# Filling TensorE with identity transposes at the start of a fused AdaLN block, with the gate modulation, one statistic and one exponential moved

## The chip, the core and the metric

The kernel runs on one core of a Trainium2 chip. The metric is the device time of one execution in microseconds (us), as the median of several runs. TensorE (PE) multiplies matrices, PEld is its loading of weights, VectorE is DVE, ScalarE is ACT, GpSimd is POOL, and SP issues most of the DMAs.

## What is computed

The input x has 8 samples of 256 rows with 128 features. It goes through eight layers of linear attention with a feed-forward part, and then through a mixture of 8 experts (top 2) with a shared one. Both halves are modulated by a small product of the condition c.

```python
mod = (silu(c) @ wmod).reshape(8, 6, 1, 128)      # shifts, scales and gates
sa, ca, ga, sb, cb, gb = the six parts of mod
h = layernorm(x) * (1 + ca) + sa                  # the input of the first layer
for layer in range(8):
    q, k, v = h @ Wq + bq, h @ Wk + bk, h @ Wv + bv
    Q, K = elu(q) + 1, elu(k) + 1
    V = Q * sum(K * v) / (Q * sum(K) + eps)       # the sums run over the rows of a sample
    h1 = layernorm(gelu(V @ Wo + bo) + h)
    h = layernorm(gelu(gelu(h1 @ Wf1 + bf1) @ Wf2 + bf2) + h1)
x = x + ga * h
out = x + gb * mixture(layernorm(x) * (1 + cb) + sb)
```

## The kernel before, in words

The 2048 rows are cut into four chunks of 512 (two samples each). Features lie on the partitions for the products, rows for the norms, so each norm is a set of four 128x128 transposes to rows, statistics and normalization on DVE, a reciprocal root on POOL (`rstd`, L1013), and four transposes back. All of it is fp32; from the fourth chunk on, the q, k and v products are made of three products of split operands.

The layers run as a software pipeline of slots (`slots`, L223). In slot s, chunk s mod 4 of its layer makes its k, q and v products (index `a` in the code), while chunk s-1 makes its denominators, its output product and first sum (`b`), chunk s-2 its feed-forward part (`f`) and chunk s-3 its last norm (`d`). Slots 0 to 2 are written out and are called the fill here; a hardware loop then runs four slots per iteration. Each engine has its own `slot` function, a list of work in a fixed order with semaphore waits. What belongs to the start alone (the input norm "I" of each of the four chunks) is passed to the slots as named extras, which a slot runs at a named place.

Around the change, engine by engine:

- **PE** (L340 to L351): ten products of zeros (L343), then with the modulation weights there `modulate(ps_y, (0, 1))`, four identity transposes (`keep_awake`, L326, whose output nobody reads), the four transposes of chunk 0's input (`first_to_fm(0)`, L319), then a wait for the gate weights and the four gate products `modulate(ps_d, (2, 3, 4, 5))` (L336). Slot 0 makes k, q and v (L360) and then `first_to_fm(1)`. Slot 1 makes k, q and v of chunk 1 (k waits for the keys of chunk 0, q for `elu_q`, v for `kv_ready`), `first_to_fm(2)`, the output product of chunk 0 (L466) and twelve identity transposes. Slot 2 starts with the transposes of y1 and chunk 2's products.
- **ACT** (L791 on): `first_norm(c)` (L768) scales and shifts chunk c's input to xs; a slot makes `lden` (L803) and `dd` (L812) for chunk s-1 and the exponentials `ek` (L808) and `eq` (L815) for chunk s, in the order lden, ek, dd, eq; then come the gelus (L821, L827), which need another activation table.
- **DVE** (L1215 on): before slot 0, statistics of chunks 0, 1 and 2 (L1117) and the normalization (L1153) of chunks 0 and 1. A slot makes `nck` (L1229), `vt` (L1240, from dd and nck), `mk` (L1250), the keys `kk` (L1258), `mq` (L1263), `elu_q_sb` (L1271), `kv_full` (L1212) and `rk` (L1290). In slot 0 the extra "before the last norm", ahead of bk1 and mk, is `first_stats(3)`; in slot 1 the same place holds `third_norm` (normalization of chunk 2, then the variance of chunk 3).
- **POOL** makes `kpos` and `qk` (L1037, L1039) once `elu_q_sb` is there, and the sum y1 (L1033) once ACT has g1.

The extras before the change read:

```python
slots(pe, slot, {"middle": lambda: first_to_fm(1)}, ...
slots(dve, slot, {"before the last norm": lambda: first_stats(CH - 1)}, ...
```

Of the kernel before, what the change touches and what calls it, by code (L numbers as in the profile page):

```python
# [7 lines left out]
ACT = mybir.ActivationFunctionType  # L8
# [10 lines left out]
CH = NB * L // G  # L19
# [12 lines left out]
def adaln_block(nc, x, w_qkv, w_o, w_f1, w_f2, v_a, v_bo, v_ln1, v_bf1, v_bf2, v_ln2, c_t, w_mod,  # L32
                w_router, w_unit, ident_in, select_in, lower_in, out):

    with ExitStack() as ctx:
        def sb(name, shape, dt=F32):
            return ctx.enter_context(nc.sbuf_tensor(name, shape, dt))

        def sem(name):
            return ctx.enter_context(nc.semaphore(name))  # L40
# [23 lines left out]
        lden, dd = sb("lden", [P, G]), sb("dd", [P, G])  # L64
# [14 lines left out]
        c_eps, c_lneps, c_half = sb("c_eps", [P, 1]), sb("c_lneps", [P, 1]), sb("c_half", [P, T])  # L79
# [34 lines left out]
        ps_k, ps_q, ps_v, ps_f0, ps_f1, ps_b, ps_d, ps_y = bank  # L114
# [9 lines left out]
        def gates(i):  # L124
# [5 lines left out]
        ld = {k: sem(f"ld_{k}") for k in ("const", "ct", "mod", "gates", "moe", "wqkv", "va", "wo", "vbo", "vln1",  # L130
                                          "wf1", "vbf1", "wf2", "vbf2", "vln2")}
# [9 lines left out]
        lden_ready, dd_ready, v_ready = sem("lden_ready"), sem("dd_ready"), sem("v_ready")  # L141
# [37 lines left out]
        def rows_of(k, n):  # L179

            return hf[n][:].rearrange("p (t d) -> p t d", t=T) if k == "I" else xh[k][:]
# [8 lines left out]
        def splits_next(s, c):  # L190

            return c == CH - 1 and not (isinstance(s, int) and s == NI - 1)

        def has(n):

            return not isinstance(n, int) or 0 <= n < NI
# [10 lines left out]
        def run(extra, place):  # L207

            if extra and place in extra:
                extra[place]()  # L210
# [12 lines left out]
        def slots(eng, one_slot, *extras):  # L223

            extras = extras + (None,) * (CH - 1 - len(extras))
            for s in range(CH - 1):
                one_slot(s, s % CH, s // CH, extras[s])
            with eng.Fori(0, LAYERS - 1) as i:  # L230
                for j in range(CH):
                    s = CH - 1 + j
                    one_slot(i * CH + s, s % CH, i + s // CH)
            one_slot(NI - 1, CH - 1, LAYERS - 1)
# [79 lines left out]
        def _(pe):  # L314
            def transposes(out_bank, src, done):

                for j in range(T):
                    t = src[:, j, :] if len(src.shape) == 3 else src[:, j * P:(j + 1) * P]
                    mm = nc.tensor.transpose(out_bank[:, j * P:(j + 1) * P], t, ident[:])  # L319
                mm.then_inc(done, 1)  # L320


            def keep_awake(n, out_bank):

                for _ in range(n):
                    nc.tensor.transpose(out_bank[:, 0:P], ident[:], ident[:])  # L326

            def first_to_fm(c):
                pe.wait_ge(normed["I"], c + 1)
                if c == CH - 1:  # L330
                    pe.wait_ge(mod_copied, 2)
                transposes(first_bank[c], rows_of("I", c), to_fm["I"])

            def modulate(out_bank, ms):
                for m in ms:
                    mm = nc.tensor.matmul(out_bank[:, m * NB:(m + 1) * NB], wmod[:, m * D:(m + 1) * D], sct[:],  # L336
                                          start=True, stop=True)
                mm.then_inc(mod_mm, 1)
# [6 lines left out]
            pe.wait_ge(ld["mod"], 16)  # L345
            pe.wait_ge(silu_c, 1)
            modulate(ps_y, (0, 1))
            keep_awake(4, ps_v)
            first_to_fm(0)
            pe.wait_ge(ld["gates"], 16)  # L350
            modulate(ps_d, (2, 3, 4, 5))  # L351

            def slot(s, c, l, extra=None):
                a, b, f, d = s, s - 1, s - 2, s - 3
# [139 lines left out]
            def second_fill():  # L494
                pe.wait_ge(mod_copied, 1)
                keep_awake(12, ps_y)

            slots(pe, slot, {"middle": lambda: first_to_fm(1)},
                  {"behind the products": lambda: first_to_fm(2), "before ff2": second_fill},
                  {"behind the products": lambda: first_to_fm(CH - 1)})  # L500

# [1 line left out]
            last = NI - 1  # L503
# [248 lines left out]
        def _(act):  # L752
# [19 lines left out]
            def split_qkv_hi(l):  # L772
                act.wait_ge(ld["wqkv"], 16 * l + 16)
                wait(act, v_mm, CH * l)
                nc.scalar.activation(wqkv_hi[:], wqkv[:], ACT.Copy).then_inc(wq_hi_ready, 1)
# [8 lines left out]
            def last_norm(c, d):  # L784
                act.wait_ge(to_fm["D"], d + 1)
                if (c - 3) % CH == 0:
                    act.wait_ge(ld["vln2"], 4 * d + 16)
                nc.scalar.activation(xs[(c - 3) % CH][:], ps_d[:], ACT.Identity,
                                     bias=vln2[:, 1:2], scale=vln2[:, 0:1]).then_inc(x_ready, 1)

            def slot(s, c, l, extra=None):  # L791
                a, b, f, d = s, s - 1, s - 2, s - 3
                if has(d):
                    act.wait_ge(ff2_mm, d + 1)
                    if (c - 3) % CH == 0:
                        act.wait_ge(ld["vbf2"], 4 * d + 16)
                    nc.scalar.activation(g2[:], ps_f0[:], ACT.Gelu_apprx_tanh, bias=vbf2[:, 0:1]).then_inc(g2_ready, 1)  # L797
                run(extra, "start")
                if (has(a) or has(b)) and not (isinstance(s, int) and s <= 1):
                    nc.scalar.preload_act_table_set(LN_SET)  # L800
                if has(b):
                    act.wait_ge(q_ready, b + 1)
                    nc.scalar.activation(lden[:], qk[:], ACT.Ln, bias=c_eps[:, 0:1]).then_inc(lden_ready, 1)  # L803
                if has(a):
                    act.wait_ge(k_mm, a + 1)
                    if c == 0:
                        act.wait_ge(ld["va"], 4 * a + 16)
                    nc.scalar.activation(ek[:], ps_k[:], ACT.Exp, bias=va[:, 0:1]).then_inc(ek_ready, 1)  # L808
                if has(b):
                    act.wait_ge(lden_ready, b + 1)  # L810

                    nc.scalar.activation(dd[:], lden[:], ACT.Exp, bias=c_lneps[:, 0:1], scale=-1.0).then_inc(dd_ready, 1)  # L812
                if has(a):
                    act.wait_ge(q_mm, a + 1)
                    nc.scalar.activation(eq[:], ps_q[:], ACT.Exp, bias=va[:, 1:2]).then_inc(eq_ready, 1)  # L815
                run(extra, "before the gelus")
                if has(b):
                    act.wait_ge(wo_mm, b + 1)
                    if (c - 1) % CH == 0:
                        act.wait_ge(ld["vbo"], 4 * b + 16)  # L820
                    nc.scalar.activation(g1[:], ps_b[:], ACT.Gelu_apprx_tanh, bias=vbo[:, 0:1]).then_inc(g1_ready, 1)  # L821
                for j in range(FJ):
                    if has(f):
                        act.wait_ge(ff1_mm, 4 * f + (2, 3, 1, 4)[j])
                        if j == 0 and (c - 2) % CH == 0:
                            act.wait_ge(ld["vbf1"], 4 * f + 16)
                        nc.scalar.activation(hid[:, j, :], ps_ff[j][:], ACT.Gelu_apprx_tanh,  # L827
                                             bias=vbf1[:, j:j + 1]).then_inc(h_ready, 1)
                    if j == 0:
                        run(extra, "after the first gelu")  # L830
                    if j == 1:
                        run(extra, "middle")
                    if j == 3:
                        run(extra, "before the last norm")
                    if j == 3 and has(a) and splits_next(s, c):
                        split_qkv_hi(l + 1)
                    if j == 3 and has(d) and has(b) and has(s + 1):
                        last_norm(c, d)
                        if has(s + 1):
                            act.wait_ge(v_mm, d + 1)  # L840
                            nc.scalar.activation(xs_hi[(c - 3) % CH][:], ps_d[:], ACT.Identity,
                                                 bias=vln2[:, 1:2], scale=vln2[:, 0:1]).then_inc(x_hi_ready, 1)
                run(extra, "end")
# [111 lines left out]
            for i in range(CH * U):  # L955
# [17 lines left out]
                if i == U + 5:  # L973
                    act.wait_ge(to_fm["D"], NI)
                    nc.scalar.activation(xs[CH - 1][:], ps_d[:], ACT.Identity,
                                         bias=vln2[:, 1:2], scale=vln2[:, 0:1]).then_inc(x_ready, 1)
# [15 lines left out]
            for h in range(HB):  # L992
                nc.scalar.activation(half(yf, h), half(ps_y, h), ACT.Copy,
                                     scale=gt[:, 1, NB - HB + h:NB - HB + h + 1]).then_inc(yf_ready, 1)
# [117 lines left out]
        def _(dve):  # L1112
# [72 lines left out]
            def first_stats(c):  # L1185
                dve.wait_ge(ld["x0"][c], 16)
                stats_of_rows("I", c, x0[:, c])
# [108 lines left out]
            def second_split():  # L1296
                split_qkv_lo(0)
                gates()

            slots(dve, slot, {"before the last norm": lambda: first_stats(CH - 1)},  # L1300
                  {"before the last norm": third_norm, "behind the keys": gates_copied,
                   "within the first norm": lambda: first_norm(CH - 1)},
                  {"behind the keys": second_split})
# [239 lines left out]
```

## Time and profile before

| what | us |
|---|---|
| median of three runs | 517.22 |
| the three runs | 515.99, 517.22, 517.27 |
| the profiled execution, its own time | 515.97 |
| its span in the profile | 514.2 |

The profile tells of the one execution of 515.97 us, whose span of 514.2 us leaves 1.8 us around it. Busy times of an engine are shares of that span. "Granted clock" is TensorE's clock as a share of 2.4 GHz: 1.00 is 2.4 GHz and 0.50 is 1.2 GHz. All times below are counted from the span's start.

### The profile page before, as it was taken

The page shows a single profiled execution, that of the slowest core. Times are in us where ns is not written, and L with a number is a line of the kernel's source. Part 1 is how long each engine was busy: PE and PEld are TensorE (multiplying, and loading weights), DVE is VectorE, ACT ScalarE, POOL GpSimd, SP SyncE. Part 2 cuts the span into 40 slices and gives each one's busy share as a digit, 9 for nine tenths or more (in the row PEclk, how much of TensorE's full clock was granted, in tenths as well). Part 3 has the DMA queues.
Part 4 walks back from the last instruction along what each step waited for, and adds up shares of the span by engine and source line. Part 5 has one row for each costly group of instructions (what it writes and reads, how often), then busy time and mean ns, then how long its engine had stood idle before and what let it go on. Part 6 is the DMA issues. An engine that isn't in the chain of part 4 may idle for free.

```text
span 514.2 us, 8044 instructions
## 1 busy us (share of the span) xinstructions
PE 500.5 (97%) x1925; PEld 299.0 (58%) x1925; DVE 425.4 (83%) x1625; ACT 389.7 (76%) x586; POOL 261.2 (51%) x306
## 2 busy tenths in 40 slices
PE   8889999999999999999999999999998999999997
PEld 6445555555555555555555555555555566766675
DVE  6888888988898888888888988898888677886854
ACT  3868888888888887888888888888897953445353
POOL 3445555556655656666555566556563450213253
PEclk8999999999999999999999999999999999999999
DMA  8200010001000100010010001000000000707070
GB/s 240 104 17 1 7 42 15 0 5 41 15 5 3 38 15 5 21 35 1 5 41 15 0 5 41 15 5 20 21 1 1 1 1 0 165 20 185 1 186 20
DMA packets 19526, 17.51 MB, mean 34 GB/s; under 512 B 8604, under 2 KB 14236, under 8 KB 19508
## 3 DMA queue, kind: packets, MB, share of 16 engines
q1 hardware_dynamic: 18644, 16.58, 12.6%
q10 hardware_dynamic: 864, 0.73, 0.5%
q8 instruction: 7, 0.11, 0.1%
q14 instruction: 11, 0.09, 0.1%
HBM read 9.96 MB, written 1.05 MB: 21 GB/s over the span
## 4 chain that ended last, share of the span: by engine, by line
PE 87%; DVE 5%; ACT 3%; issue 2%; POOL 2%; DMA 1%; DVEq 0%; POOLq 0%
PE bank L453 19%; PE bank L444 14%; PE bank L319 12%; PE bank L466 5%; PE bank L607 5%; PE bank L441 5%; PE bank L361 4%; PE bank L366 4%; PE bank L362 4%; PE bank L564 3%; PE bank L565 3%; PE bank L566 3%; PE bank L666 1%; DVE hf L1153 1%; PE bank L673 1%
## 5 line engine op out<-in xcount | busy, mean ns | idle before, releaser
L453 PE MATMUL bank<-hid,wf 128*128 128x512 f32 x240 | 112.9, 592 | 0.0
L1013 POOL TENSOR_TENSOR rsD<-veD,c_half 128x4 f32<-128x4 f32 x32 | 37.8, 1180 | 119.5 <-DVE veD L1134 119.5
L444 PE MATMUL bank<-x,wf 128*128 128x512 f32 x180 | 87.2, 593 | 0.0
L827 ACT ACTIVATE hid<-bank,vbf 128x512 f32<-128x512 f32 x120 | 72.5, 693 | 0.0
L453 PEld LDWEIGHTS bank<-hid,wf 128*128 128x128 f32 x240 | 43.1, 190 | 43.2 <-issue 29.0
L444 PEld LDWEIGHTS bank<-x,wf 128*128 128x128 f32 x180 | 32.8, 189 | 31.8 <-DVE kk L1258 15.1
L1153 DVE TENSOR_SCALAR xhB<-bank,meanB,rsB 128x128 f32<-128x128 f32 x128 | 43.7, 404 | 8.6 <-POOL rsB L1013 8.6
L1224 DVE TENSOR_SCALAR x<-bank,vln 128x256 f32<-128x256 f32 x60 | 29.9, 539 | 22.4 <-PE bank L319 22.4
L1153 DVE TENSOR_SCALAR xhD<-bank,meanD,rsD 128x128 f32<-128x128 f32 x128 | 43.7, 404 | 5.4 <-POOL rsD L1013 1.1
L797 ACT ACTIVATE g<-bank,vbf 128x512 f32<-128x512 f32 x29 | 20.0, 689 | 34.8 <-PE bank L453 34.8
L319 PEld LDWEIGHTS bank<-ident,y 128*128 128x128 f32 x256 | 29.4, 140 | 27.2 <-POOL y L1033 12.4
L361 PE MATMUL bank<-xs_hi,wqkv_hi 128*128 128x512 f32 x87 | 43.7, 502 | 0.8
L1013 POOL TENSOR_TENSOR rsB<-veB,c_half 128x4 f32<-128x4 f32 x32 | 32.8, 1025 | 19.6 <-DVE veB L1134 19.6
L1033 POOL TENSOR_TENSOR y<-g,xs 128x512 f32<-128x512 f32 x31 | 39.5, 1273 | 4.5 <-ACT g L821 4.4
L319 PE MATMUL bank<-ident,y 128*128 128x128 f32 x256 | 39.6, 278 | 0.8 <-POOL y L1033 0.8
L821 ACT ACT_TABLE_LOAD x31 | 39.8, 1283 | 0.6
L1021 POOL TENSOR_TENSOR xs_lo<-xs,xs_hi 128x512 fp32r<-128x512 f32 x29 | 38.4, 1323 | 2.5 <-ACT xs_hi L779 2.5
L800 ACT ACT_TABLE_LOAD x30 | 38.5, 1283 | 0.6
L564 PE MATMUL bank<-xs_hi,wu_hi 128*128 128x512 f32 x76 | 37.9, 498 | 0.3 <-DVE sc L1459 0.3
L1028 POOL TENSOR_TENSOR y<-g,x 128x512 f32<-128x512 f32 x29 | 37.2, 1283 | 0.2 <-ACT g L797 0.2
L366 PE MATMUL bank<-xs_lo,wqkv_hi 128*128 128x512 f32 x87 | 34.6, 452 | 0.0
L362 PE MATMUL bank<-xs_hi,wqkv_lo 128*128 128x512 f32 x87 | 34.4, 396 | 0.0
(204 smaller groups left out, 1150.4 us busy)
## 6 DMA issues: line engine op xcount, KB each, us to landing
wf<-in_w_f SPq DMA_DIRECT2D x16, 256.0 KB, 2.6
hid<-kv_full SPq DMA_DIRECT2D x12, 256.0 KB, 4.3
x<-kv_full SPq DMA_DIRECT2D x9, 256.0 KB, 4.9
wu<-in_w_unit SPq DMA_DIRECT2D x10, 192.0 KB
wqkv<-in_w_qkv SPq DMA_DIRECT2D x7, 192.0 KB, 2.4
x<-in_x SPq DMA_DIRECT2D x4, 256.0 KB, 5.4
qk<-kv_full SPq DMA_DIRECT2D x3, 256.0 KB, 4.9
out<-ot SPq DMA_DIRECT2D x3, 256.0 KB, 2.6
```

The source lines that it names most:

```text
L319: mm = nc.tensor.transpose(out_bank[:, j * P:(j + 1) * P], t, ident[:])
L361: nc.tensor.matmul(bank[:], wqkv_hi[:, w], xs_hi[c][:], start=True, stop=False)
L362: return nc.tensor.matmul(bank[:], wqkv_lo[:, w], xs_hi[c][:], start=False, stop=False)
L366: return nc.tensor.matmul(bank[:], wqkv_hi[:, w], xs_lo[c][:], start=False, stop=True)
L444: mm = nc.tensor.matmul(ps_ff[j][:], wf1[:, j * P:(j + 1) * P], x2[(c - 2) % CH][:], start=True, stop=True)
L453: mm = nc.tensor.matmul(ps_f0[:], wf2[:, j, :], hid[:, j, :], start=(j == 0), stop=(j == FJ - 1))
L564: nc.tensor.matmul(bank[:], wu_hi[:, u, m, :], h_hi[c % 2][:], start=True, stop=False)
L821: nc.scalar.activation(g1[:], ps_b[:], ACT.Gelu_apprx_tanh, bias=vbo[:, 0:1]).then_inc(g1_ready, 1)
L827: nc.scalar.activation(hid[:, j, :], ps_ff[j][:], ACT.Gelu_apprx_tanh, bias=vbf1[:, j:j + 1]).then_inc(h_ready, 1)
L1013: nc.gpsimd.tensor_tensor(rs[buf(k, n)][:], ve[buf(k, n)][:], c_half[:], ALU.pow).then_inc(rstd_ready[k], 1)
L1033: nc.gpsimd.tensor_tensor(y1[:], g1[:], xs[(c - 1) % CH][:], ALU.add).then_inc(y1_ready, 1)
L1153: ap = nc.vector.tensor_scalar(rows_of(k, n)[:, j, :], src[:, j, :], mean[q][:, j:j + 1], rs[q][:, j:j + 1], ALU.subtract, ALU.mult)
```

## The change

PE makes seven identity transposes in place of four ahead of `first_to_fm(0)`, and eleven more behind it, where the gate products were. The gate products, with their wait for the gate weights, go behind `first_to_fm(1)`, in the middle of slot 0. On ACT, in slot 1 alone, dd goes ahead of ek. On DVE `first_stats(3)` goes from ahead of slot 0's keys to behind its sum of keys and values ("behind the keys"). No other slot changes.

```diff
--- before.py
+++ after.py
@@ -345,10 +345,14 @@
             pe.wait_ge(ld["mod"], 16)
             pe.wait_ge(silu_c, 1)
             modulate(ps_y, (0, 1))
-            keep_awake(4, ps_v)
+            keep_awake(7, ps_v)
             first_to_fm(0)
-            pe.wait_ge(ld["gates"], 16)
-            modulate(ps_d, (2, 3, 4, 5))
+            keep_awake(11, ps_v)
+
+            def second_input():
+                first_to_fm(1)
+                pe.wait_ge(ld["gates"], 16)
+                modulate(ps_d, (2, 3, 4, 5))
 
             def slot(s, c, l, extra=None):
                 a, b, f, d = s, s - 1, s - 2, s - 3
@@ -495,7 +499,7 @@
                 pe.wait_ge(mod_copied, 1)
                 keep_awake(12, ps_y)
 
-            slots(pe, slot, {"middle": lambda: first_to_fm(1)},
+            slots(pe, slot, {"middle": second_input},
                   {"behind the products": lambda: first_to_fm(2), "before ff2": second_fill},
                   {"behind the products": lambda: first_to_fm(CH - 1)})
 
@@ -801,15 +805,24 @@
                 if has(b):
                     act.wait_ge(q_ready, b + 1)
                     nc.scalar.activation(lden[:], qk[:], ACT.Ln, bias=c_eps[:, 0:1]).then_inc(lden_ready, 1)
-                if has(a):
+
+                def keys():
                     act.wait_ge(k_mm, a + 1)
                     if c == 0:
                         act.wait_ge(ld["va"], 4 * a + 16)
                     nc.scalar.activation(ek[:], ps_k[:], ACT.Exp, bias=va[:, 0:1]).then_inc(ek_ready, 1)
+
+                def denominators():
+                    act.wait_ge(lden_ready, b + 1)
+                    nc.scalar.activation(dd[:], lden[:], ACT.Exp, bias=c_lneps[:, 0:1], scale=-1.0).then_inc(dd_ready, 1)
+
+                second = isinstance(s, int) and s == 1
+                if has(a) and not second:
+                    keys()
                 if has(b):
-                    act.wait_ge(lden_ready, b + 1)
-
-                    nc.scalar.activation(dd[:], lden[:], ACT.Exp, bias=c_lneps[:, 0:1], scale=-1.0).then_inc(dd_ready, 1)
+                    denominators()
+                if has(a) and second:
+                    keys()
                 if has(a):
                     act.wait_ge(q_mm, a + 1)
                     nc.scalar.activation(eq[:], ps_q[:], ACT.Exp, bias=va[:, 1:2]).then_inc(eq_ready, 1)
@@ -1297,7 +1310,7 @@
                 split_qkv_lo(0)
                 gates()
 
-            slots(dve, slot, {"before the last norm": lambda: first_stats(CH - 1)},
+            slots(dve, slot, {"behind the keys": lambda: first_stats(CH - 1)},
                   {"before the last norm": third_norm, "behind the keys": gates_copied,
                    "within the first norm": lambda: first_norm(CH - 1)},
                   {"behind the keys": second_split})
```

## Rows read from the trace of the kernel before

**Rows 1.** The page, busy time, share of the span and instructions of TensorE.
```profile
PE 500.5 (97%) x1925; PEld 299.0 (58%) x1925; DVE 425.4 (83%) x1625; ACT 389.7 (76%) x586; POOL 261.2 (51%) x306
```

**Rows 2.** Busy time in stretches: stretch, length, engines, granted clock, DMA share, GB/s.
```profile
0.00:30.00 30.00, 23.70 (x97) 15.42 (x98) 22.42 (x101) 18.66 (x27) 11.84 (x25) 0.94 0.48 147
...
60.00:120.00 60.00, 59.88 (x227) 34.03 (x226) 52.42 (x218) 51.28 (x72) 35.34 (x40) 1.00 0.06 18
```

**Rows 3.** The chain that ended last, 0 to 50 us: start, length, what.
```profile
10.84 1.03 DVE hf L1153 x4
11.86 0.78 DVE stI L1117 x4
...
15.09 0.89 DVE kv_full L1212 x4
...
16.22 0.47 issue
16.70 1.11 DVE hf L1153 x4
...
22.35 0.67 PE bank L319 x4
...
23.05 0.90 DVE stB L1117 x4
...
39.35 0.66 PE bank L319 x4
```

**Rows 4.** TensorE in order of time, 6.6 to 23 us: start, us, line, idle before.
```profile
6.68 0.63 PE L326 MATMUL bank<-ident 128*128 128x128 f32 x4
7.56 0.66 PE L319 MATMUL bank<-ident,hf 128*128 128x128 f32 x4 [0.24 <-DVE hf L1153]
8.10 1.06 PE L336 MATMUL bank<-sct,wmod 128*128 128x8 f32 x8
9.39 4.54 PE L360 MATMUL bank<-xs,wqkv 128*128 128x512 f32 x6 [0.23 <-ACT xs L768]
...
15.48 2.84 PE L360 MATMUL bank<-xs,wqkv 128*128 128x512 f32 x6 [1.11 <-ACT xs L768]
...
19.10 1.12 PE L466 MATMUL bank<-vt,wo 128*128 128x512 f32 x2 [0.34 <-DVE vt L1240]
20.06 1.47 PE L326 MATMUL bank<-ident 128*128 128x128 f32 x12
```

**Rows 5.** Busy time and granted clock in stretches of the fill, columns as in rows 2.
```profile
6.70:9.90 3.20, 2.73 (x19) 2.06 (x19) 3.06 (x19) 1.02 (x2) 0.59 (x1) 1.00 1.07 322
9.90:13.30 3.40, 3.40 (x5) 1.35 (x4) 3.18 (x17) 1.24 (x2) 1.54 (x2) 0.50 0.92 251
...
19.60:22.80 3.20, 2.38 (x18) 1.82 (x17) 2.71 (x11) 3.12 (x5) 1.77 (x3) 1.00 0.00 0
22.80:25.40 2.60, 2.60 (x8) 1.00 (x6) 2.25 (x13) 2.34 (x5) 1.29 (x3) 1.00 0.00 0
```

**Rows 6.** ScalarE in order of time, in the first 45 us.
```profile
12.74 0.69 ACT L815 ACTIVATE eq<-bank,va 128x512 f32<-128x512 f32 x1 [0.97 <-PE bank L360]
...
17.61 0.71 ACT L812 ACTIVATE dd<-lden,c_lneps 128x512 f32<-128x512 f32 x1
...
20.26 0.69 ACT L821 ACTIVATE g<-bank,vbo 128x512 f32<-128x512 f32 x1
```

**Rows 7.** GpSimd and VectorE in order of time, in the first 45 us.
```profile
10.84 1.12 POOL L1013 TENSOR_TENSOR rsI<-veI,c_half 128x4 f32<-128x4 f32 x1 [0.51 <-DVE veI L1134]
...
15.43 0.94 POOL L1039 TENSOR_SCALAR qk<-elu_q_sb,ksum 128x256 f32<-128x256 f32 x2
...
16.16 0.22 DVE L1229 SCALAR_TENSOR_TENSOR nck<-kvsum,rk 128x2 f32<-128x2 f32 x1
...
18.27 0.16 DVE L1141 SCALAR_TENSOR_TENSOR meanI<-difI,stI 128x4 f32<-128x4 f32 x1
...
18.43 0.62 DVE L1240 TENSOR_SCALAR vt<-dd,nck 128x256 f32<-128x256 f32 x2
```

More of the change, by code:

```diff
@@ L808, in slot @@
                     nc.scalar.activation(ek[:], ps_k[:], ACT.Exp, bias=va[:, 0:1]).then_inc(ek_ready, 1)
-                if has(b):
+                def denominators():
                     act.wait_ge(lden_ready, b + 1)
                     nc.scalar.activation(dd[:], lden[:], ACT.Exp, bias=c_lneps[:, 0:1], scale=-1.0).then_inc(dd_ready, 1)
+                second = isinstance(s, int) and s == 1
+                if has(a) and not second:
+                    keys()
+                if has(b):
+                    denominators()
+                if has(a) and second:
+                    keys()
                 if has(a):
```

## The prediction

> **What bounds the kernel now.** I read the page first: TensorE is busy for 97% of the span [rows 1]. Then the stretches: in the first 30 us it is busy for 23.70 of 30.00 us, and from 60 to 120 for 59.88 of 60.00 [rows 2]. So the loop is bound by TensorE, and what the change can move lies in the fill. The chain of waits says where the fill ends: from 39.35 us on all of it is TensorE, before that it runs over VectorE, GpSimd and ScalarE [rows 3]. A microsecond won or lost on that chain ahead of 39.35 us is won or lost in the end; one won elsewhere is not.
>
> In the part that the change touches the chain is VectorE's own list: the normalization of chunk 1 from 10.84 us, the statistics of chunk 3 from 11.86, kv_full of slot 0 from 15.09 to 15.98, a gap of 0.47 us, the normalization of chunk 2 from 16.70 [rows 3]. TensorE's fall in clock (0.50 of full speed from 9.90 to 13.30, [rows 5]) is not on it: slot 0's exponential eq ends at 12.74 + 0.69 = 13.43 us [rows 6], while the chain has VectorE on other work until past that.
>
> One measure for all that follows: 0.3% of 517.22 is 1.55 us, about what a measurement of this kernel can tell from no change.
>
> **Seven transposes for four.** Twelve take 1.47 us, and four 0.63 us [rows 4], so one more costs (1.47 - 0.63) / 8 = 0.105 us and three cost 0.32. TensorE stands idle for 0.24 us at that place, waiting for VectorE's normalization [rows 4]. At worst the transposes of chunk 0 come 0.1 us late. The cover is VectorE, which does not look at slot 0's products before 11.86 us. Priced at 0; the cover gone, 0.1 us.
>
> **Gate products out, eleven transposes in.** Out go 1.06 us, in come 11 x 0.105 = 1.16. The next work, the k product, starts at 9.39 us after 0.23 us of idle time [rows 4], so it starts at 9.4 to 9.5. Same cover, 0.
>
> **The clock of slot 0's products.** Six matmuls took 4.54 us in slot 0, and 2.84 in slot 1 at 1.00 [rows 4]. If the clock stays up, v ends 1.7 us earlier, at 12.2 us instead of 13.9. This is the largest number in the change, and I credit nothing for it: k is then ready at 10.4 us and q at 11.3, but VectorE comes to them at 11.86, when the normalization of chunk 1 ends [rows 3].
>
> **Gate products behind chunk 1's transposes.** In slot 0 their 1.06 us stand ahead of slot 1's k product, with a wait for the gate weights. Behind that wait on TensorE's queue is all of slot 1; who waits for it is ScalarE's ek and VectorE's sums. Before, the products ran at 8.10 us without idle time [rows 4], so the weights were there by then and the wait is free. The transposes end at about 12.6 us, and ScalarE then needs its time for xs of chunk 1, which k needs as well: it is the 1.11 us for which TensorE is idle ahead of 15.48 [rows 4], and the gate products take its place. 0. The copy out of their bank comes at the end of slot 1 on VectorE as before, far behind.
>
> **Statistics of chunk 3 moved (0.78 us, [rows 3]).** Without them VectorE starts mk at 11.9 us in place of 12.7, and keys, elu_q_sb and kv_full all come 0.78 us earlier: kv_full ends at 15.2 instead of 15.98. Then it does the statistics, until 15.98. The list up to rk and nck holds the same work without a hole in either order, so nck starts at 16.16 as before. What the move gives is the inputs of others: slot 1's q and v products, and GpSimd's qk, go 0.7 to 0.8 us earlier. The input rows of chunk 3 landed before 11.86 us, so no DMA is at stake, and no queue issues another transfer for this change.
>
> **dd ahead of ek.** qk now ends at 16.37 us and would end at about 15.6 [rows 7]. lden follows (an exponential's 0.7 us), then dd from 16.3 to 17.0 instead of 17.61 to 18.32 [rows 6]. But vt needs VectorE as well: the last small operation ahead of it starts at 18.27, and vt at 18.43 [rows 7]. So 1.3 us on ScalarE buy 0 to 0.07 us of vt. ek goes behind it, from 17.0 to 17.7; mk of slot 1, which reads it, stands behind vt, which ends at 19.05. The output product follows vt (19.10), g1 that product (20.26), then y1, the transposes at 22.35 and the statistics at 23.05. The product ends at 20.22 us, so g1 moves with vt and no more. Here nothing further is released: a faster ScalarE meets a VectorE with no hole left.
>
> **The unknowns.** (a) nck took 0.22 us, ending as GpSimd's qk ends (16.38 and 16.37 us) [rows 7]; with qk earlier it may take 0.16, as the small operation at 18.27 does: 0.06 gained, or nothing. (b) The hole ahead of the normalization of chunk 2, 0.47 us in the chain and 0.31 of real idle time, has no releaser in the trace. It may go (0.31 gained) or stay, being at the same place of the same list. I take it as staying, since nothing that ends late stands ahead of it in either kernel. (c) mk now starts while GpSimd still works on a reciprocal root, from 10.84 to 11.96 us [rows 7], and may be held as nck was: 0.1 lost or nothing. Sum: from 0.1 lost to 0.45 gained, taken at 0.1 gained, the 0.07 of vt with (a) and (c) about even. The profiled execution of 515.97 us would become 515.9. It lies 1.25 below the median of 517.22, two of three runs being near the latter; the same 0.1 off the median gives **517.1 us**.
>
> **Rival 1: the fall stays, as transposes do not hold the clock.** For: eight transposes stood in the stretch from 6.70 to 9.90 us, and the fall came right behind it [rows 5]. Against: from 20.2 to 22.8 us TensorE did nothing but sixteen transposes [rows 3, 4], and the stretch behind it still has 1.00 [rows 5]. In this case slot 0's matmuls take 4.5 us again, q is ready at 12.7, mq waits for eq until 13.45, about 0.25 us longer than the list needs, and the list is late by that: 517.2 + 0.2 = 517.4 us. The Trainium skill states such a rule ("TensorE: Matmul & The Clock Gate", Part 4: PE-mode transpose): transposes are not counted as activity and do not bring the fast clock. By this rule the sum would be this rival's and not the forecast's; the rows from 20.2 us on speak against it. This is also the case in which the change doesn't do what it says. Chance 0.12.
>
> **Rival 2: the fall moves, slower.** TensorE saves its 1.7 us, yet has nothing to put there. Slot 1's products would run from 13.8 to about 16.3 us instead of 15.48 to 18.32, and chunk 2's transposes can't start before VectorE's normalization of 16.70 to 17.81. So between 16.3 and 19.1 us TensorE has 0.6 us of transposes and else is idle, where before it was at products until 18.3 [rows 4]. If the clock falls behind that hole, what runs at half speed is the output product (0.86 us more), or the twelve transposes (1.3 more, of which the idle time ahead of 22.35 takes 0.8), and y1's four (0.45 more): 0.45 to 0.9 us at the statistics of 23.05, and at most 1.6 with all of them. It decides from the point at which the clock falls between 18 and 22 us. For: the stretch that was followed by the fall, 6.70 to 9.90, was itself busy for 2.73 of 3.20 us [rows 5], with eight transposes and products of eight columns, so light work was enough for it. Against: idle time and four transposes between 13.9 and 15.48 us brought no fall. Taken at 0.8: 517.2 + 0.8 = 518.0 us. Chance 0.20.
>
> **Rival 3: more than the sum.** The hole (b) goes, so that dd's early end pays: 0.45 us. And the new kernel's executions lie at the low one of the two levels of before (515.99, and 517.22 with 517.27), if what parts these levels is a fall of the clock that the filling prevents. 515.99 - 0.45 = 515.5 us. The trace shows one execution, so nothing speaks for or against the second half. Chance 0.18.
>
> **The numbers.** The forecast, 0.50, with its own range of 515.9 to 517.4. The range reaches from rival 3 to rival 2: 515.5 to 518.1. Faster by over 0.3% (under 515.67) is nearly all of rival 3: 0.17. Slower by over 0.3% (over 518.77) takes the upper end of rival 2 on top of a high level: 0.06. Within 0.3%: 0.77.
>
> **What would show it.** Right: granted clock 1.00 from 9.9 to 13.3 us; mk of slot 0 at 11.9 and kv_full ended by 15.3; dd ended at 17.0 and vt still at 18.3 to 18.4; statistics of y1 at 23.0; the chain all TensorE from about 39.2. Wrong: 0.50 at the same place (rival 1); 0.50 anywhere between 18 and 24 us, with statistics of y1 after 23.4 (rival 2); vt before 18.1 us (the hole gone), or the start of the all-TensorE chain moved by over 1 us, which would mean that a wait that I do not see in the fill was set by TensorE.

## The result and the profile after

In the first comparison the changed kernel took 517.83 us (median of 9 executions, 516.15 to 518.12), the kernel before 516.20 (9 executions, 515.96 to 517.27). The ratio is 1.002, with a 95% interval of 1.001 to 1.0029: slower by 0.2%. The forecast was 517.1 us against a median of 517.22 that rested on three executions, two of them high ones.

The executions of the changed kernel lie at two levels: seven at 517.8 to 518.1 us, with a mean granted clock of 0.992 or 0.993, and two at 516.15 and 516.16 with 1.00. An execution is called high here if it is over 516.6 us, and low otherwise. Wherever the clock was recorded, high executions of either kernel have 0.997 or less, and none with 0.998 or more is high. The reverse does not hold: 37 of 85 low executions of the kernel before have 0.997 too. The profiled execution of the changed kernel is a high one, of 518.12 us. First its page and its stretches, columns as in [rows 1] and [rows 2].

```profile
PE 503.6 (98%) x1939; PEld 301.6 (58%) x1939; DVE 426.4 (83%) x1625; ACT 390.1 (76%) x586; POOL 260.7 (50%) x306
```

```profile
0.00:30.00 30.00, 24.12 (x109) 16.89 (x110) 21.64 (x99) 18.31 (x27) 12.06 (x25) 0.94 0.48 147
30.00:60.00 30.00, 29.65 (x100) 16.17 (x99) 26.12 (x106) 22.35 (x33) 14.42 (x17) 0.94 0.04 10
60.00:120.00 60.00, 59.87 (x226) 34.03 (x225) 52.63 (x218) 51.27 (x72) 35.36 (x40) 1.00 0.06 14
```

TensorE is as full as before from 60 us on. Its busy time rose by 3.1 us, though the matmuls that it got are fourteen transposes (1.5 us); the rest is clock. The granted clock was 0.94 in the first 30 us before as well; new is 0.94 in the next 30. TensorE in order of time, columns as in [rows 4]:

```profile
6.47 0.96 PE L326 MATMUL bank<-ident 128*128 128x128 f32 x7
7.69 0.66 PE L319 MATMUL bank<-ident,hf 128*128 128x128 f32 x4 [0.26 <-DVE hf L1166]
8.18 1.36 PE L326 MATMUL bank<-ident 128*128 128x128 f32 x11
9.52 2.84 PE L364 MATMUL bank<-xs,wqkv 128*128 128x512 f32 x6
12.20 0.60 PE L319 MATMUL bank<-ident,hf 128*128 128x128 f32 x4
12.63 0.96 PE L336 MATMUL bank<-sct,wmod 128*128 128x8 f32 x8
13.91 2.84 PE L364 MATMUL bank<-xs,wqkv 128*128 128x512 f32 x6 [0.32 <-ACT xs L772]
18.00 0.66 PE L319 MATMUL bank<-ident,hf 128*128 128x128 f32 x4 [1.25 <-DVE hf L1166]
19.15 1.57 PE L470 MATMUL bank<-vt,wo 128*128 128x512 f32 x2 [0.49 <-DVE vt L1253]
20.51 2.74 PE L326 MATMUL bank<-ident 128*128 128x128 f32 x12
```

The change did what it says: slot 0's products take 2.84 us instead of 4.54, slot 1's start at 13.91 instead of 15.48. Then TensorE waits 1.25 us for VectorE's normalization and 0.49 for vt. Behind that the output product takes 1.57 us for 1.12, and the twelve transposes 2.74 for 1.47 [rows 4]. Stretches of the same execution, clock behind the five engines:

```profile
16.70:19.70 3.00, 1.26 (x7) 0.73 (x7) 2.76 (x13) 2.98 (x4) 1.12 (x1) 1.00 0.02 7
19.70:23.10 3.40, 3.40 (x15) 2.77 (x14) 2.66 (x11) 2.33 (x4) 1.58 (x3) 0.50 0.00 0
...
26.40:29.90 3.50, 1.80 (x10) 1.26 (x11) 2.61 (x8) 2.77 (x6) 1.03 (x2) 1.00 0.00 0
29.90:33.40 3.50, 3.50 (x7) 1.78 (x7) 3.39 (x11) 0.65 (x1) 0.35 (x1) 0.51 0.00 0
```

There are two falls to 1.2 GHz, each behind a stretch in which TensorE was busy about half the time or less. For the first, that stretch is new. The nearest stretch of the kernel before was nearly full, since slot 1's products ran until 18.32 us:

```profile
16.35:19.75 3.40, 3.06 (x11) 1.48 (x10) 2.98 (x14) 3.32 (x5) 1.03 (x2) 1.00 0.07 25
```

The first fall is on the output product, the twelve transposes and the transposes of y1; the second on the feed-forward products of slot 2. The chain that ended last shows what they cost; here the twelve transposes, work that nobody reads, stand on it.

```profile
16.83 1.12 DVE hf L1166 x4
...
19.15 1.57 PE bank L470 x2
20.72 2.54 PE bank L326 x12
23.26 0.45 PE bank L319 x4
23.71 0.02 issue
23.73 0.90 DVE stB L1130 x4
...
41.17 0.66 PE bank L319 x4
```

The statistics of y1 start at 23.73 us, for 23.05 before [rows 3], and the part that is all TensorE (the entry, below) starts at 41.17 instead of 39.35. So 1.8 us are lost in all, 0.7 by 23.7 us and 1.1 behind it. Next come the prediction's other steps: VectorE, GpSimd and ScalarE in order of time.

```profile
11.97 0.42 DVE L1263 TENSOR_SCALAR mk<-ek 128x512 f32<-128x512 f32 x1
...
16.29 0.16 DVE L1242 SCALAR_TENSOR_TENSOR nck<-kvsum,rk 128x2 f32<-128x2 f32 x1
16.83 1.12 DVE L1166 TENSOR_SCALAR hf<-x,meanI,rsI 128x128 f32<-128x128 f32 x4 [0.38 <-issue]
18.48 0.61 DVE L1253 TENSOR_SCALAR vt<-dd,nck 128x256 f32<-128x256 f32 x2
```

```profile
14.79 0.94 POOL L1052 TENSOR_SCALAR qk<-elu_q_sb,ksum 128x256 f32<-128x256 f32 x2
```

```profile
15.77 0.72 ACT L807 ACTIVATE lden<-qk,c_eps 128x512 f32<-128x512 f32 x1 [1.91 <-POOL qk L1052]
16.52 0.72 ACT L817 ACTIVATE dd<-lden,c_lneps 128x512 f32<-128x512 f32 x1
```

dd ends at 17.24 us instead of 18.32, vt starts at 18.48 instead of 18.43 [rows 7]. The hole ahead of chunk 2's normalization is still there (0.38 us idle).

### The profile page after: what moved, and what is told of

It reads as the page before. It is cut to its first block, busy times and chain, and to the rows that moved or that the text cites. A ratio compares the mean times of both kernels' runs of the same rounds, so it can differ in the third digit from the quotient of the medians.

```text
span 516.3 us, 8072 instructions
## 1 busy us (share of the span) xinstructions
PE 503.6 (98%) x1939; PEld 301.6 (58%) x1939; DVE 426.4 (83%) x1625; ACT 390.1 (76%) x586; POOL 260.7 (50%) x306
## 4 chain that ended last, share of the span: by engine, by line
PE 87%; DVE 5%; ACT 3%; issue 2%; POOL 1%; DMA 1%; DVEq 0%; POOLq 0%
PE bank L457 19%; PE bank L448 14%; PE bank L319 12%; PE bank L470 6%; PE bank L611 5%; PE bank L445 5%; PE bank L365 4%; PE bank L370 4%; PE bank L366 4%; PE bank L568 3%; PE bank L570 3%; PE bank L569 3%; PE bank L670 1%; DVE hf L1166 1%; PE bank L677 1%
## 5 line engine op out<-in xcount | busy, mean ns | idle before, releaser
L1237 DVE TENSOR_SCALAR x<-bank,vln 128x256 f32<-128x256 f32 x60 | 29.9, 540 | 22.4 <-PE bank L319 22.4
L319 PEld LDWEIGHTS bank<-ident,y 128*128 128x128 f32 x256 | 29.6, 141 | 26.1 <-POOL y L1046 11.4
L470 PE MATMUL bank<-vt,wo 128*128 128x512 f32 x62 | 34.7, 642 | 0.5 <-DVE vt L1253 0.5
```

The source lines that it names most:

```text
L470: nc.tensor.matmul(ps_b[:], wo[:], vt[(c - 1) % CH][:], start=True, stop=True).then_inc(wo_mm, 1)
```

## The experiments

Two theories stood first. **C**: the loss is falls of TensorE's clock, behind idle time that the earlier end of slot 1's products opens. **D** and **E**: TensorE's new order (D), or the moves on the other engines (E), cost the time by themselves. Kernels that were measured side by side share their executions of the kernel before ("the same" in the table). "High" is the count over 516.6 us. e8 has one execution and stands in its own part below.

| run | median us | high | before beside it, high | ratio and interval |
|---|---|---|---|---|
| first comparison, changed | 517.83 | 7 of 9 | 2 of 9 | 1.002 (1.001 to 1.0029) |
| e1 TensorE's part | 516.15 | 2 of 12 | 13 of 35 | 0.9993 (0.9983 to 1.0004) |
| e2 moves only | 516.06 | 3 of 12 | the same | 0.9994 (0.9984 to 1.0004) |
| e3 slot 1 filled | 516.08 | 3 of 12 | the same | 0.9993 (0.9984 to 1.0003) |
| e4 no eleven | 516.11 | 4 of 12 | the same | 1.0 (0.9989 to 1.0011) |
| e5 changed | 516.02 | 3 of 11 | 11 of 27 | 1.0001 (0.9989 to 1.0013) |
| e6 slots 1 and 2 filled | 516.05 | 0 of 11 | the same | 0.9993 (0.9984 to 1.0002) |
| e7 before, slot 2 filled | 516.22 | 0 of 11 | the same | 0.9992 (0.9983 to 1.0002) |
| e9 changed, slot 2 filled | 516.08 | 0 of 11 | 12 of 35 | 0.9992 (0.9983 to 1.0001) |
| e10 changed, no twelve | 516.51 | 6 of 12 | the same | 1.0005 (0.9995 to 1.0016) |
| e11 before, no twelve | 517.62 | 10 of 11 | the same | 1.0021 (1.0012 to 1.0031) |
| e12 changed | 516.20 | 4 of 12 | the same | 1.0003 (0.9994 to 1.0013) |
| e13 changed | 516.10 | 3 of 11 | 5 of 29 | 1.0 (0.9992 to 1.0009) |
| e14 changed | 516.28 | 5 of 12 | the same | 1.0011 (1.0001 to 1.0022) |
| e15 no twelve, slot 2 filled | 516.57 | 6 of 12 | the same | 1.0011 (1.0 to 1.0022) |

**One part alone: e1 and e2.** e1 has TensorE's part of the diff and e2 the ScalarE and VectorE parts.

> TensorE's part of the change alone (7 and 11 transposes, gate products behind chunk 1's transposes); ScalarE and VectorE as before. Theory C: the 1.6 us lost are falls of TensorE's clock behind the idle time from 16.8 to 19.2 us. With VectorE's statistics still ahead of the keys, slot 1's q and v products wait 0.8 us longer, end at about 17.5 us, and the idle time ahead of the output product shrinks to some 1.2 us: most executions without a fall near 20 us, 516.2 us. Theory D: the new place of the gate products or the transposes themselves cost the time, whatever the other engines do: 517.8 us.

> The moves on ScalarE (dd ahead of ek) and VectorE (statistics of chunk 3 behind the keys) alone; TensorE's list as before. Theory C: the clock falls at about 9.9 us as before, slot 0's products end at 13.9, slot 1's run from 15.5 to 18.2, no idle time arises ahead of 20 us: 516.1 us. Theory E: the order of the moved work delays vt or y1: 517.8 us, with y1's statistics at 23.7.

Neither part is slower than the kernel before, so D and E fall as far as they say that an order costs 1.7 us each time. (What a part does to the level of its few high executions is not told by two and three of them.) e1's idle time came as forecast: slot 1's products end at 17.52 us, and TensorE then waits 0.65 and 0.57 us. In e2 the fall that I had expected at 9.9 us was not in the profiled execution, its slot 0 ran at full clock, and the idle time in slot 1 was there too:

```profile
18.12 0.66 PE L319 MATMUL bank<-ident,hf 128*128 128x128 f32 x4 [1.15 <-DVE hf L1162]
```

**Filling slot 1, and taking the eleven out: e3 and e4.**

```diff
+            def third_input():
+                pe.wait_ge(mod_copied, 1)
+                keep_awake(11, ps_y)
+                first_to_fm(2)
+                keep_awake(5, ps_y)
...
-                  {"behind the products": lambda: first_to_fm(2), "before ff2": second_fill},
+                  {"behind the products": third_input, "before ff2": second_fill},
```

```diff
             first_to_fm(0)
-            keep_awake(11, ps_v)
```

> The changed kernel with 11 more identity transposes behind slot 1's products and 5 behind chunk 2's. Theory C, if transposes hold the clock: no fall at 19.7 us; y1's statistics at 23.0; the second fall, at 29.9 us, may stay where it was: 516.2 us, or 517.0 with it. Theory C, if transposes don't hold it: 517.8. Theories D and E: 517.8.

> The changed kernel without the eleven transposes ahead of slot 0's products; gate products stay at their new place. If transposes hold the clock: it falls at about 9.5 to 10 us as before the change, slot 0's products end near 14 us, slot 1's near 18, the idle time ahead of the output product is gone: 516.2 us. If transposes count for nothing (rival 1 of the prediction): the same falls and the same time as the changed kernel, 517.8 us.

Neither told what it was meant to tell, since the kernel before beside them was high as often: the level of one execution is drawn anew each time, and twelve executions say little on a share. What e3 adds is where its high executions lie: 517.07, 517.15 and 517.42, the level of the kernel before, and none at 517.8. Three are few to go by. e4's profiled execution had no fall near 9.9 us although the eleven were gone, so at that place they are not needed each time, and e4 does not tell whether they count. After these I stopped reading medians and counted executions.

**The changed kernel again, and slot 2 filled: e5, e6, e7.** Slot 2's part, on the changed kernel with e3's part (e6) and on the kernel before (e7):

```diff
-                  {"behind the products": lambda: first_to_fm(CH - 1)})
+                  {"behind the products": fourth_input, "start": lambda: keep_awake(6, ps_y)})
...
+            def fourth_input():
+                first_to_fm(CH - 1)
+                keep_awake(8, ps_y)
```

> The changed kernel itself, for the share of its executions at each level. Theory C (falls of the clock after the idle time ahead of the output product): a large part, a third to three quarters of the executions, at 517.1 to 518.1 us with a granted clock of 0.997 or less, the rest at 516.1; where the clock is 1.00 the time is 516.1. Theory F (the earlier comparison caught the two kernels at different moments): about as many high executions as the kernel before has, one in three.

> The changed kernel with 11 and 5 transposes in slot 1 and 8 and 6 more in slot 2, around the transposes of the first inner norm, so that TensorE has no idle time of over 0.8 us between 6 and 40 us. Theory C: all executions, or all but one, at 515.9 to 516.4 us with clock 1.00. If the high level has another cause than falls after light work: one execution in four at 517.1 as with the hole of slot 1 alone filled.

> The kernel before with the 8 and 6 transposes in slot 2 alone. Theory C: the high level of the kernel before (517.1, one execution in three) comes from a fall near 26 to 30 us, ahead of or in the feed-forward products; filling the idle time there takes most of it away: at most one execution in ten over 516.6 us, median 516.1. If it comes from falls in slot 0 and 1: still one in three.

e5's profiled execution is a low one (515.94 us), and the best test of the working: the changed kernel without a fall. TensorE in order of time, then the chain, then the stretches that answer to the two falls above.

```profile
19.09 1.12 PE L470 MATMUL bank<-vt,wo 128*128 128x512 f32 x2 [0.48 <-DVE vt L1253]
20.05 1.47 PE L326 MATMUL bank<-ident 128*128 128x128 f32 x12
```

```profile
23.04 0.90 DVE stB L1130 x4
...
39.35 0.66 PE bank L319 x4
```

```profile
19.70:23.10 3.40, 2.58 (x19) 1.99 (x18) 2.66 (x12) 2.83 (x4) 2.09 (x4) 1.00 0.00 0
...
26.40:29.90 3.50, 1.85 (x10) 1.44 (x10) 2.78 (x9) 3.35 (x5) 1.26 (x1) 1.00 0.00 0
29.90:33.40 3.50, 3.50 (x9) 1.47 (x8) 3.43 (x14) 1.82 (x4) 1.06 (x1) 1.00 0.00 0
```

Statistics of y1 at 23.04 us and entry at 39.35: the kernel before to 0.01 us [rows 3]. All of the change's gain on TensorE is spent waiting for VectorE. From 16.7 to 19.7 us TensorE was busy here for 1.27 of 3.00 us, and from 26.4 to 29.9 for 1.85 of 3.50, as little as in the execution with the two falls (1.26 and 1.80), and the clock stayed up. The kernel before has the same 1.85 of 3.50 in its trace, without a fall. So the light stretches come before the falls but do not bring one each time. e6 and e7 came out as theory C has them: none of 22 executions high, where the kernel before had 11 of 27. For the kernel before this is how its high level is known to hang on the filling of slot 2; no trace of a high execution of it was kept, so where its clock falls in one was not seen. e6 on TensorE:

```profile
16.66 1.36 PE L326 MATMUL bank<-ident 128*128 128x128 f32 x11
...
26.38 1.04 PE L326 MATMUL bank<-ident 128*128 128x128 f32 x8
...
27.96 0.82 PE L326 MATMUL bank<-ident 128*128 128x128 f32 x6
28.85 1.10 PE L445 MATMUL bank<-x,wf 128*128 128x256 f32 x4
```

The feed-forward products start right behind the last filling transposes, at 28.85 us, as late as without them (28.72 in e5, whose whole list ran about 0.13 us earlier by then). So the filling delayed nothing that can be seen.

**Do transposes count for the clock? e8.**

```diff
-            for _ in range(10):
-                nc.tensor.matmul(ps_v[:, 0:P], zeros, zeros, start=True, stop=True)
...
-            keep_awake(4, ps_v)
+            keep_awake(100, ps_v)
```

> The kernel before without the ten products of zeros and with 100 identity transposes in place of four: TensorE makes nothing but transposes and two small gate products (8 columns) for over 10 us. If transposes count as work for the clock: it rises during them and stays up, their pitch goes from 0.21 to 0.11 us, time 516 + about 11 = 527 us. If they don't (rival 1): granted clock 0.50 through all of them, the pitch stays at 0.21, and the time is 516 + about 21 = 537 us.

It took 525.60 us (one execution). The count of matmuls in each stretch is the pace of transposes:

```profile
5.60:8.60 3.00, 3.00 (x16) 3.00 (x16) 2.14 (x10) 0.47 (x1) 0.70 (x1) 1.00 1.10 367
8.60:11.60 3.00, 3.00 (x25) 3.00 (x24) 2.79 (x18) 0.00 (x0) 1.74 (x2) 1.00 0.91 249
11.60:14.60 3.00, 3.00 (x30) 3.00 (x29) 1.13 (x7) 0.00 (x0) 0.39 (x1) 1.00 0.94 294
```

Sixteen in 3 us, then 25, then 30: the pace doubles while TensorE makes nothing but transposes, and stays. (The clock column says 1.00 throughout; it knows no level ahead of the first change that was recorded, so here the pace is the witness.) The time is 1.4 us from the first case and 11.4 from the second. Identity transposes both raise the clock and hold it.

**Slot 2 alone, and fewer transposes in slot 1: e9, e10, e11, e12.** e9 is the changed kernel with slot 2's part; e10 and e11 are the changed kernel and the kernel before with this edit; e12 is the changed kernel.

```diff
             def second_fill():
                 pe.wait_ge(mod_copied, 1)
-                keep_awake(12, ps_y)
```

> The changed kernel with the 8 and 6 transposes of slot 2 alone; the idle time of slot 1 stays. Theory C, with the two falls of the changed kernel priced apart: a fall near 20 us still comes in a quarter to a half of the executions and costs 0.7 us, the one near 30 us (1.1 us) is gone: high executions at 516.7 to 517.0 us, none at 517.8. If the fall near 30 us is not prevented by filling: 517.8 again. If slot 1's idle time alone brings no fall: all at 516.1.

> The changed kernel without the twelve transposes behind the output product of chunk 0: from 16.8 to 22.3 us TensorE then has four transposes and one product. Theory C: the fall, now and then in the changed kernel, becomes the rule: two thirds of the executions or more over 516.6 us, median 517 to 518.5. If light work ahead is not what brings the falls: no more high executions than the changed kernel has.

> The kernel before without the same twelve. It has products until 18.3 us, then the same four transposes and one product, and is idle from 20.2 to 22.3 us. Theory C: more high executions than its one in three, fewer than the changed kernel without the twelve; median 516.2 to 517.3 us. If light work ahead is not what brings the falls: one in three.

> The changed kernel once more, for the share of high executions (7 of 9 at first, 3 of 11 the second time). If the change makes falls more common: 4 or more of 11 to 12, those that are high mostly at 517.8 to 518.1. If the first comparison caught a rare moment: 3 or 4, as the kernel before beside it.

e9: none high, the slowest 516.60 us with a clock of 0.996. The expected quarter to half of the executions at 516.7 to 517.0 did not come; that is the outcome which the expectation gave to "no fall from slot 1's idle time alone". But slot 2's transposes run after 20 us and can't prevent a fall there, and if a quarter of the executions had one, none in eleven would still come once in 24 times. So e9 does not tell whether that fall comes alone, and the price of 0.7 us for it was not measured. e11 shows that light work brings falls: without the twelve transposes the kernel before goes from 12 of 35 high to 10 of 11. e10 does not show it. The changed kernel without the twelve has 6 of 12, beside 4 of 12 with them (e12), and I had expected more from it than from e11. In e10's profiled execution (516.34 us), TensorE is idle for 2.21 us ahead of y1's transposes and still keeps its clock:

```profile
22.66 0.63 PE L319 MATMUL bank<-ident,y 128*128 128x128 f32 x4 [2.21 <-DVE mod L1180]
```

Why e11 is worse than e10 stays open. e12 has 4 of 12, which fits both of its cases: two at 517.75 and 517.96, and two at 516.83 and 516.89 with a clock of 0.997. The latter lie where one fall that costs 0.7 us would put them; no trace shows it.

**What was still open: e13, e14, e15.** e13 and e14 are the changed kernel; e15 is e10 with slot 2's part.

> The changed kernel, to count executions over 516.6 us: 14 of 32 so far, the kernel before 38 of 106. Theory G (the change makes falls more common, as 7 of 9 said): half or more of this and the next run together. Theory F (the first comparison caught a rare moment; the change alters what a bad execution costs, 1.7 us for 1.1, and not how many there are): about one in three, most of them at 517.8 to 518.1.

> As the run before it; the two are counted together. Theory G: 12 or more of some 23 over 516.6 us. Theory F: 5 to 11.

> The changed kernel without the twelve transposes of slot 1 and with the 8 and 6 of slot 2: the fall near 20 us is made likely, the one near 30 us prevented, so that the first is priced by itself. If the two falls add up (0.7 and 1.1 us): high executions at 516.6 to 517.2 us, none at 517.8. If idle time in slot 1 makes late falls by itself: 517.2 to 518 as without the filling.

e13 and e14 together have 8 of 23 high: theory F's count. Beside them the kernel before has only 5 of 29, and e14 alone is slower again (1.0011, interval 1.0001 to 1.0022), so a somewhat higher share is not excluded. e13's profiled execution (517.66 us) is a second trace with the two falls, taken on another chip than e5's. Its chain:

```profile
19.06 1.61 PE bank L470 x2
20.67 2.50 PE bank L326 x12
23.17 0.45 PE bank L319 x4
23.62 0.02 issue
23.64 0.90 DVE stB L1130 x4
...
41.07 0.66 PE bank L319 x4
```

The same: 0.6 us at the statistics of y1 against e5, 1.7 at the entry. e15 missed. With slot 2 filled it still had executions of 517.71, 517.78 and 518.58 us, so by these counts (0 of 11 in e9, 6 of 12 here) filling slot 2 protects only as long as slot 1 has its twelve; the fall near 20 us has no measured price of its own beyond what the chains show.

All executions of the changed kernel and of the kernel before, over the five comparisons of the former and e1 to e4: 22 of 55 high (40%) against 43 of 135 (32%). Low executions have the same median, 516.06 and 516.10 us. High ones do not: 517.80 against 517.24, with 14 of 22 at 517.7 or more against 2 of 43. The means are 516.71 and 516.48 us, 0.23 us apart with a standard error of 0.12. Much of that is the first comparison: without it they are 516.55 and 516.49, and 15 of 46 beside 41 of 126 are high.

## Why the prediction was right or wrong

**The base.** It was set by a median of three executions, two of them high. The larger sample puts the kernel before at 516.2. The prediction noted the two levels and did not ask how many executions are at each, which decides the median. Its case for rival 2, 517.2 + 0.8 = 518.0 us, comes near the measured 517.83 by luck: the base was 1.0 too high, and its price of 0.8 us was 1.0 too low (a high execution lost 1.7 to 1.8 us in the traces).

**The working of the parts was right.** Seven and eleven transposes, the gate products' new place: 0, as e5 shows (entry at 39.35 in both). (The wait for the gate weights is not free at the old place in each execution: in e2 the gate products were idle for it for 0.37 us, at 8.84 us. At the new place no trace shows it.) The clock of slot 0's products: 1.7 us saved on TensorE, credited with nothing, and worth nothing. The kernel before shows the same without the change. The two traces with a fall near 9.9 us, before and e7, have a mean granted clock of 0.997; e11's and e2's, with TensorE's start as before, have no such fall, 2.84 and 2.82 us for slot 0's products, and a clock of 1.00. Of the 85 low executions of the kernel before with a recorded clock, 37 have 0.997 and 48 have 0.998 or more; their medians are 516.09 and 516.11 us. So, as far as the mean clock tells, the fall that the change was to remove is absent from about half of them anyway, and costs nothing where it comes. mk at 11.97 us for a forecast 11.9; vt at 18.48 (18.42 in e5) for 18.3 to 18.4. dd ended at 17.24, not 17.0, without effect. Unknown (a), nck's duration: 0.16 us as supposed, and not seen in the end. Unknown (b): the hole stayed. Together the forecast gain of 0.1 us is a low median of 516.06 for 516.10, no more than noise.

**The step that failed: the idle time that the change opens on TensorE stands in the sum at nothing.** The sum has VectorE as the cover of all that TensorE gains, and leaves out that TensorE's clock may fall behind the new idle time and put TensorE itself on the chain. In the first comparison 7 of 9 executions lay at 517.8 us or more, and the profiled one of them was 1.8 us late at the entry, against a forecast of 0.1 us gained. The mechanism was not unseen. Rival 2 has it, with its idle time, the work that runs at half speed and the price at the statistics of y1 (0.45 to 0.9 us; measured 0.69 and 0.60), but with a chance of 0.20 and outside the sum. Its working had three faults. First, it has no second fall. In both traces the clock falls again at 29.9 us, on feed-forward products that are on the way to the entry: 1.1 us more, and the "at most 1.6", meant for the first fall alone, became 1.8. Why the second came is open: the stretch ahead of it is as light without the first (1.85 of 3.50 us in e5), only 0.7 us earlier. Second, it has slot 1's products end at about 16.3 us; 2.84 us from 13.91 end at 16.75, and TensorE's idle time came to 1.25 + 0.49 = 1.74 us where 2.2 follow from its numbers. Third, it treats a fall as something that a kernel has or has not. It is a share of executions: in the first comparison 7 of 9, in the four later ones 15 of 46. That the first comparison caught 7 of 9 is in part chance, and "slower by 0.2%" is that comparison's, not the kernel's: over all executions the means are 0.04% apart, which is not clear of noise. About half of it is the higher price of a high execution and half their larger share (22 of 55 beside 43 of 135); that the share rises is not shown.

**Rival 1 fell, and with it the rule.** The Trainium skill ("TensorE: Matmul & The Clock Gate", Part 4: PE-mode transpose) says that transposes aren't counted as activity. This case's trace does not agree: in e8 the pace rises to that of the full clock (30 transposes in 3 us instead of 16) during fp32 identity transposes alone. The measurement decides: here they count. In the traces of the changed kernel (after, e5, e13) slot 0's products behind the eleven transposes take 2.84 us, but e4 had that without them, so no run shows that the eleven were needed.

**Rival 3** was half right: the 1.1 us between the levels of the kernel before go with a lower granted clock, and filling in slot 2 takes the high level away (e6, e7, e9: none of 33 high, beside 23 of 62 of the kernel before and 7 of 23 of the changed one). It is not the fall at 9.9 us, which the change was to remove. What rival 3 made of it did not come: 7 of 9 executions of the changed kernel were high, and the hole (b) stayed, with 0.38 us of idle time for 0.31.

**What would be better** than both kernels: e6 or e9 at 516.05 and 516.08 us median. The median gains 0.03% at most, within noise; the mean goes from 516.5 or more to 516.03 (e6) and 516.06 (e9), because the high executions are gone. e7 shows that the change is not needed for it: the kernel before with slot 2 filled has none high either, and a mean of 516.21.

## What to carry to other kernels

Here, work that TensorE did earlier only moved its idle time, and the new place mattered: the clock fell there in some executions, and what followed came onto the chain. Fill the idle time ahead of the products on the critical chain, not the one ahead of products that somebody else covers. Where executions lie at levels, count them: a median of nine can be all of one level, and an interval around it does not know that the next nine may be of the other.

## What the runs showed that was not expected

- Two falls come together: both traces with a fall near 19.7 us have a second one near 29.9 us (29.93 and 29.80 us). That the first brings the second is not shown; by the counts of e7 the kernel before has falls that filling slot 2 prevents, with no new idle time in slot 1.
- Filling transposes become the critical path once the clock is down: twelve took 2.74 us instead of 1.47, and in both traces with that fall they stood on the chain (2.54 and 2.50 us of it).
- Idle time of 2.21 us did not bring a fall in one execution (e10), while one came behind 1.25 and 0.49 us with four transposes between them in another; the same kernel (e5) had 1.25 and 0.48 us and no fall. What decides it in one execution was not found. The share could be moved, down by filling slot 2 (none of 33) and up by taking the twelve transposes out of the kernel before (10 of 11).
- A hole of 0.3 to 0.4 us of idle time on VectorE ahead of chunk 2's normalization stands in every trace that was read for it, whatever precedes it. Its cause was not sought.
